# Banded attention in one program: a separate norm stage against one folded in, new engine orders, turned values

## The reference

```
x = x + attn_b(layernorm(x))           # 16 heads of 64
q = rmsnorm(x @ wq.T, q_gamma)         # over all 1024 columns of a token
k = rmsnorm(x @ wk.T, k_gamma);  v = x @ wv.T
scores = q k^T / 8 + slope_h * (j - i) # masked unless -128 <= j - i <= 0
out = softmax(scores) @ v;  attn_b = out @ wo.T
```

## Time and profile before

| what | us |
|---|---|
| median of three runs | 4155.57 |
| the three runs | 4155.28, 4165.5, 4155.57 |
| the profiled execution | 4160.83 |
| its span, first to last instruction | 4158.8 |
| TensorE busy / loads | 3639.6 / 2872.0 |
| VectorE, ScalarE, GpSimd busy | 2451.2, 1842.3, 780.7 |

### The profile page before, as it was taken

The page is one execution under the profiler, slowest core; times in us unless marked ns, Lnnn a source line. Parts: engine busy times, 40 slices in busy tenths (PEclk is TensorE's granted clock), DMA queues, the critical chain, the costliest instruction groups (busy, mean ns, idle before and its releaser), DMA issues. The chain is left out here.

```text
span 4158.8 us, 91975 instructions
## 1 busy us (share of the span) xinstructions
PE 3639.6 (88%) x33000; PEld 2872.0 (69%) x33000; DVE 2451.2 (59%) x5269; ACT 1842.3 (44%) x3752; POOL 780.7 (19%) x714
## 2 busy tenths in 40 slices
PE   4899999999966969999947899888989787899998
PEld 3566666666655858888835777777777676788887
DVE  4566666666645666666544545444545566666664
ACT  1466666666622324444413444444444232344443
POOL 0122222222210013333210000000000000233332
PEclk9999999999987979999969999999999788899999
DMA  4565556555534234333240000000000232343432
GB/s 178 145 172 170 174 172 173 168 171 174 169 123 150 86 119 122 110 108 117 75 142 33 13 13 12 13 13 13 13 13 15 87 118 93 117 122 111 115 110 44
DMA packets 383709, 424.97 MB, mean 102 GB/s; under 512 B 172864, under 2 KB 323008, under 8 KB 369728
## 3 DMA queue, kind: packets, MB, share of 16 engines
q1 hardware_dynamic: 358720, 386.04, 29.2%
q0 software_dynamic: 24576, 33.57, 4.6%
HBM read 269.24 MB, written 150.27 MB: 101 GB/s over the span
## 5 line engine op out<-in xcount | busy, mean ns | idle before, releaser
L2212 ACT ACTIVATE a_prob<-a_ps_s,a_low 128x512 f32<-128x512 f32 x512 | 318.9, 689 | 48.5 <-DVE a_low L2404 47.5
L2073 PE MATMUL a_ps_p<-a_ident,a_prob 128*128 128x128 f32 x2048 | 311.0, 285 | 14.9 <-ACT a_band L2192 9.0
L2404 DVE TENSOR_REDUCE a_low<-a_ps_s 128x2 f32<-128x1024 f32 x256 | 313.5, 1224 | 8.8
L2264 POOL TENSOR_TENSOR a_below<-a_probT,a_upper 128x512 f32<-128x512 f32 x128 | 164.3, 1284 | 726.4 <-ACT a_probT L2188 371.2
L2073 PEld LDWEIGHTS a_ps_p<-a_ident,a_prob 128*128 128x128 f32 x2048 | 217.7, 141 | 108.6 <-issue 83.3
L2188 ACT COPY a_probT<-a_ps_p 128x512 f32<-128x512 f32 x352 | 194.0, 588 | 155.6 <-PE a_ps_p L2073 155.6
L1510 ACT ACTIVATE b_prob<-b_score,b_low 128x256 f32<-128x256 f32 (+1 forms) x512 | 240.6, 473 | 23.7 <-PE b_ps_p L1452 23.7
L1462 PEld LDWEIGHTS b_ps_o<-b_v,b_probT 128*128 128x128 f32 x1792 | 227.2, 191 | 9.9 <-issue 0.9
L1583 DVE CUSTOM_DVE_ANT_0 b_score<-b_ps_s,b_bias 128x256 f32<-128x256 f32 (+1 forms) x512 | 186.0, 389 | 75.2 <-PE b_ps_s L1443 47.6
L1462 PE MATMUL b_ps_o<-b_v,b_probT 128*128 128x64 f32 x1792 | 228.2, 267 | 0.7 <-DVE b_o L1596 0.7
L2403 DVE TENSOR_TENSOR a_ps_s<-a_ps_s,a_win 128x320 f32<-128x320 f32 (+1 forms) x256 | 135.0, 527 | 140.2 <-PE a_ps_s L2106 135.7
(11 more groups left out here) (398 smaller groups left out, 10512.2 us busy)
## 6 DMA issues: line engine op xcount, KB each, us to landing
a_win<-band SPq DMA_DIRECT2D x128, 384.0 KB, 4.8
prob<-a_prob SPq DMA_DIRECT2D x128, 384.0 KB, 3.6
xnT<-n_xnT SPq DMA_DIRECT2D x32, 512.0 KB, 3.0
shift<-a_gbias SPq DMA_DIRECT2D x64, 256.0 KB, 2.4
a_shifted<-shift SPq DMA_DIRECT2D x256, 64.0 KB, 2.0
a_bins<-prob SPq DMA_DIRECT2D x128, 128.0 KB, 3.5
fe_gT<-in_WgT SPq DMA_DIRECT2D x16, 1024.0 KB
fe_uT<-in_WuT SPq DMA_DIRECT2D x16, 1024.0 KB
```

The costliest lines, as they stand in the source:

```text
L2073: last = nc.tensor.transpose(bank[:, c * P:(c + 1) * P], prob[:, t % 2, h, 32 + c * P:32 + (c + 1) * P], ident[:, :])
L2212: nc.scalar.activation(prob[:, t % 2, h, 32:32 + T], ps_s[pair][:, r, :], ACT.Exp, bias=low[:, h:h + 1]).then_inc(exped, 1)
L2264: nc.gpsimd.tensor_tensor(below[:, t % 2, :, :], probT[:, t % 2, :, t * P:(t + 1) * P], upper[:, :].unsqueeze(1).to_broadcast([P, HG, P]), ...
L2404: nc.vector.reduce_max(low[:, 2 * pair:2 * pair + 2], both[:, :, :], AX.X, negate=True).then_inc(maxed, 1)
```

## The change

- The stage n2 is no longer called. `window_stage` loads x itself, in four buffers, one a position t, and computes statistics, power, normed x, its transpose (kind `x`, through `ps_w`) and its split.
- Each of the five engines follows a list of its own, whose entries name kind, number and which tile relative to the unit's. In the place of `filled` and `emptied` there is a semaphore for each kind. The score, low and prob buffers hold eight heads instead of four.
- q and k halves: VectorE copies `ps_w` into `raw`; ScalarE squares `raw`. The two gammas are multiplied into one, `gains`, transposed at the start, and applied when VectorE empties `q_T`.
- The division by the row sum moves in front of the transposes: VectorE makes the reciprocal of two heads (`inverse`), GpSimd multiplies (`divide`), 128 x 512 at a time.
- Values: v is the weight (64 columns), the transposed probabilities stream; the output lands transposed in `ps_o`, two heads in the two halves of its partitions. `out_T` is gone. ScalarE takes the high part of the output (`high`), VectorE the rest (`rest`), and the output product is three fp32r products for each of eight chunks; wo is split for this at the start.
- Weights are split by ScalarE (high) and VectorE (rest), wo too, before the first tile's normed x. gamma is loaded as one row. The loop covers batches 2 to 6; -1 (two units), 0, 1, 7 and 8 (two units) are unrolled.

```diff
-        norm_stage(nc, "n2", ident, x2, xnT)
-        window_stage(nc, "b", ins, x2, xnT, ins["b_wqT"], ...
+        window_stage(nc, "b", ins, x2, ins["b_wqT"], ...
+WINDOW_ORDER = [
+    ("scores", 0, 0), ("x", 0, 1), ("values", 7, -1), ("scores", 1, 0), ("q", 0, 1), ("scores", 2, 0), ("out", 0, -1), ("probs_T", 0, 0),
+    ("q", 1, 1), ("probs_T", 1, 0), ("values", 0, 0), ("k", 0, 1), ("scores", 3, 0), ("k", 1, 1), ("probs_T", 2, 0), ("values", 1, 0), ("v", 0, 1),
+    ("probs_T", 3, 0), ("values", 2, 0), ("probs_T", 4, 0), ("q_T", 0, 1), ("values", 3, 0), ("probs_T", 5, 0), ("q_T", 1, 1), ("probs_T", 6, 0),
+    ("values", 4, 0), ("k_T", 0, 1), ("values", 5, 0), ("k_T", 1, 1), ("probs_T", 7, 0), ("values", 6, 0), ("v", 1, 1),
+]
+WINDOW_SCALAR_ORDER = [
+    ("x", 0, 1), ("high", 1, -1), ("exp", 0, 0), ("exp", 1, 0), ("exp", 2, 0), ("exp", 3, 0), ("q", 0, 1), ("exp", 4, 0), ("q", 1, 1), ("k", 0, 1),
+    ("exp", 5, 0), ("k", 1, 1), ("exp", 6, 0), ("v", 0, 1), ("exp", 7, 0), ("high", 0, 0), ("k_T", 0, 1), ("k_T", 1, 1), ("v", 1, 1),
+]
+WINDOW_VECTOR_ORDER = [
+    ("probs_T", 6, -1), ("x_normed", 0, 1), ("probs_T", 7, -1), ("x_stats", 0, 2), ("biased", 0, 0), ("x", 0, 1), ("biased", 1, 0),
+    ("rest", 1, -1), ("inverse", 0, 0), ("biased", 2, 0), ("q", 0, 1), ("inverse", 1, 0), ("biased", 3, 0), ("biased", 4, 0), ("out", 0, -1),
+    ("inverse", 2, 0), ("probs_T", 0, 0), ("q", 1, 1), ("inverse", 3, 0), ("x_mean", 0, 2), ("x_var", 0, 2), ("biased", 5, 0), ("k", 0, 1),
+    ("probs_T", 1, 0), ("inverse", 4, 0), ("biased", 6, 0), ("k", 1, 1), ("probs_T", 2, 0), ("inverse", 5, 0), ("mean", 0, 1), ("biased", 7, 0),
+    ("probs_T", 3, 0), ("inverse", 6, 0), ("probs_T", 4, 0), ("q_T", 0, 1), ("rest", 0, 0), ("q_T", 1, 1), ("inverse", 7, 0), ("probs_T", 5, 0),
+]
+WINDOW_POOL_ORDER = [
+    ("divide", 0, 0), ("divide", 1, 0), ("divide", 2, 0), ("x_pow", 0, 2), ("divide", 3, 0), ("divide", 4, 0), ("pow", 0, 1), ("normed", 0, 1),
+    ("divide", 5, 0), ("divide", 6, 0), ("normed", 1, 1), ("divide", 7, 0),
+]
+WINDOW_SYNC_ORDER = [("store", 0, -1), ("load", 0, 3)]
...
 # TensorE
+                elif kind == "out":
+                    pe.wait_ge(o_taken, 2 * w + 2)
+                    terms = [(c, o_part, w_part) for c in range(CH) for o_part, w_part in ((1, 0), (0, 0), (0, 1))]
+                    for c, o_part, w_part in terms:
+                        last = nc.tensor.matmul(ps_w[:, 0:C], oT[o_part][:, c, :], wo[w_part][:, c, :], ...
...
+                    elif kind == "probs_T":
+                        pe.wait_ge(divided, 8 * w + k + 1)
+                        reach(pe, copied, 8 * w + k - 1)
...
+                        for c in range(lo, 2):
+                            for r in range(2):
+                                h = 2 * k + r
+                                mm = nc.tensor.matmul(ps_o[BD * r:BD * r + BD, k % 4 * P:(k % 4 + 1) * P], v[:, at[1] - 1 + c, h * BD:(h + 1) * BD],
+                                                      probT[:, k % 2, r, c, :], start=(c == lo), stop=(c == 1), skip_group_check=True)
 # GpSimd
+                    elif kind == "normed":
+                        reach_alone(pool, pow_ready, w + 1)
+                        reach_alone(pool, raw_taken, 4 * w + 2 * k + 2)
+                        reach_alone(pool, filled["T"], 4 * w - 2 + 2 * k)
+                        nc.gpsimd.tensor_scalar(normed[:, k, :], raw[:, k, :], rrms[:, k:k + 1], 1.0, ALU.mult, ALU.mult).then_inc(normed_ready, 1)
+                    elif kind == "divide":
+                        reach_alone(pool, rinv_ready, 8 * w + k + 1)
+                        nc.gpsimd.tensor_tensor(part, part, by_row, ALU.mult).then_inc(divided, 1)
```

More of the change, by code:

```diff
@@ L1190, in _ @@
             finish(E - 1, 1, E // 2 - 1, False)
[L1193 to L1199, removed]
-WINDOW_ORDER = [
[L1206 to L1210, removed]
-]
@@ L1227, in window_stage @@
     HW = BC // HALVES
+    SECTIONS = ("x", "q", "k", "v", "q_T", "k_T", "out")
     with ExitStack() as ctx:
@@ L1287, in window_stage @@
         valued = s.sem("valued")
+        o_high = s.sem("o_high")
         o_taken = s.sem("o_taken")
         block = ctx.enter_context(s.programs())
[L1291 to L1305, removed]
@@ L1323, in section_number @@
[L1323 to L1340, removed]
@@ L1342, in uses, with tile_at, exists, steps @@
-        def uses(b, t):
-            return 2 * b + t // 2 + 1
+        def tile_at(b, t, off):
+            return b + (t + off) // NT, (t + off) % NT
+        def exists(kind, b, t):
+            return not isinstance(b, int) or 0 <= b < B
+        def steps(order, b, t):
+            for kind, k, off in order:
+                at = tile_at(b, t, off)
+                if exists(kind, *at):
+                    yield kind, k, *at
+        def rounds(engine, unit):
+            for t in range(NT - 2, NT):
+                unit(-1, t)
+            for b in range(2):
+                for t in range(NT):
+                    unit(b, t)
+            with engine.Fori(2, B - 1) as b:
+                for t in range(NT):
+                    unit(b, t)
+            for t in range(NT):
+                unit(B - 1, t)
+            for t in range(2):
+                unit(B, t)
@@ new lines, in unit @@
+            def unit(b, t):
+                for kind, _, *at in steps(WINDOW_SYNC_ORDER, b, t):
+                    if kind == "load":
+                        if not isinstance(at[0], int) or at[0] > 0 or at[1] > 1:
+                            load(*at)
+                    elif kind == "store":
+                        store(*at)
+            load(0, 0)
+            sp.dma_start(raw[0:1, :, :], gamma_d[0:1, :, :]).then_inc(gamma_in, 16)
+            for tile, dram, sem in ((ident, const["ident"], ident_in), (w_whole["q"], wqT_d, w_in["q"]),
+                                    (w_whole["k"], wkT_d, w_in["k"]), (w_whole["v"], wvT_d, w_in["v"])):
+                sp.dma_start(tile[tuple(slice(None) for _ in tile.shape)], dram).then_inc(sem, 16)
@@ new lines, in section @@
+            def section(kind, k, b, t):
+                w = number(b, t)
+                if kind == "x":
+                    pe.wait_ge(x_normed, w + 1)
+                    for c in range(KC):
+                        last = nc.tensor.transpose(ps_w[:, c * P:(c + 1) * P], xn[:, t % 2, c * P:(c + 1) * P], ident[:, :])
+                    last.then_inc(filled["x"], 1)
+                elif kind in ("q", "k", "v"):
+                    pe.wait_ge(x_split, w + 1)
+                    if isinstance(w, int) and w == 0 and k == 0:
```

498 lines of the change are left out of this document (269 added, 229 removed).

## The result

The changed kernel takes **3935.98 us** (median of 4, 3931.45 to 3943.92) beside 4155.42 for the kernel before (median of 4): a ratio of 0.9469, interval 0.9447 to 0.9492, 219 us gained where 185 were forecast. The profiled execution took 3943.92, its span is 3942.1.

What follows compares the result with a forecast made beforehand. TensorE's own program was taken to bound the kernel before, GpSimd's tail to set the pitch after. Savings of 91 (full tiles), 29 (first tiles), 7 (jumps), 55 (start) and 3 (end) sum to 185 us: median 3971, range 3920 to 4045.

Steps and rivals of the forecast that it cites:

- (a): TensorE's values product turned, two heads in two column halves: a step 0.60 us instead of 0.84, 1.9 saved a tile.
- Rival D: Column halves do not overlap: a values step stays 0.84 us, three on the path, +20, 3991 us; chance 0.09.
- rival E: Weight loads do not overlap in the turned values product: each step 1.3 us, kernel 4062; chance 0.03.
- (b), (d): TensorE, per tile: two o transposes and their ScalarE copies go (1.2 us); two x transposes are added (0.35).
- (c): Output product on TensorE as 24 fp32r products of 256 columns: about 2.85 us instead of 3.56 a tile.
- The path of a full tile: TensorE to k 1, then GpSimd's norm and divides, then TensorE: pitch 29.25 us, 3.8 saved a tile, 91 over 24.
- rival B: Divides find enough slack, only TensorE and its bank count: tiles 27.6 and 26.0 us, kernel 3922; chance 0.14.
- Rival C: GpSimd's divides are slower than their nearest row, say 2.0 us: +58, kernel 4029; chance 0.20.
- rival F: VectorE and GpSimd shut each other out of memory: divide 3.7 us, kernel about 4165, at 4 about 4190; chance 0.04.
- First tiles: First tile of each batch, with ps_w as the chain: 27.2 us against 30.78, 29 saved over eight.
- Loop jumps: Jumps of the loop over batches: 4 instead of 5, each 6.7 us in the mean, 7 saved.
- Start and end: Start: n2 goes, first scores at 42 us instead of 97.6, 55 saved; end: fewer transposes and copies, 3 saved.

Runs made afterwards that it cites:

- e3: Changed kernel with both heads of a values step writing the same half of the PSUM partitions: 4003.22 us, ratio 0.9638.
- e12: As e3, but each head's sum over its key blocks finished before the next head's began: 4006.67 us, ratio 0.9622.
- e8: Changed kernel with the output product back in f32, without the rest of o and the split of wo's rest: 3976.1 us, ratio 0.9568.
- e1: Changed kernel with each GpSimd divide treating only the first 32 columns of each head's block: 3933.76 us, ratio 0.9462.
- e2: Changed kernel with each divide done twice on GpSimd, the first into a spare buffer: 3985.61 us, ratio 0.959.
- e7: Changed kernel with the divides moved from GpSimd to VectorE, right behind each reciprocal: 3992.02 us, ratio 0.9596.
- e6: Changed kernel with its loop over batches written out: 3923.52 us, ratio 0.9432.
- e5: Kernel before the change with its loop over batches 1 to 6 written out: 4124.05 us, ratio 0.9913.
- e9: Changed kernel with the norm stage n2 put back in front of the window stage, its result unused: 3998.36 us, ratio 0.9601.
- e10: Changed kernel with 16 increments of an unused semaphore on TensorE's queue at the end of the loop body: 3938.85 us, ratio 0.947.
- e11: Changed kernel with 48 increments of an unused semaphore on TensorE's queue at the end of the loop body: 3978.62 us, ratio 0.9557.

## Why the prediction was right, and where not

**The bound.** Right: TensorE's own program sets the pace before and after, and its work per tile decides.

**(a) Values turned.** Right in mechanism and size: 0.59 for 0.60, and e3 and e12 show that the two column halves make the difference (1.02 with both heads in one). Rival D, no overlap of the halves, falls with it. So does rival E: the loads of the 64 columns last 0.136 each, eight in a step of 0.59 beside their products. The Trainium skill, page "TensorE: Matmul & The Clock Gate", section on packing small matmuls, would let them overlap only between different row groups; here the rows of the array are all in use, and the trace disagrees with it. My sum missed one thing: the four transposes ahead of a values step take 0.53, not 0.44, 0.7 us a tile.

**(b), (d).** The o transposes are gone and the x transposes cost about what was counted (the two at 2501.85 take 0.36 up to the values behind them).

**(c) Output product.** 2.92 for 2.85, in e8 0.54 less than in f32 where 0.7 were counted.

**The path of a full tile.** This step failed. "Pitch 29.25" came from GpSimd's tail; the pitch is 28.46 and comes from TensorE's work and its bank. What was mis-sized is the divide: 1.02 back to back for 1.283 + 0.27, three of them 1.6 us of the path. The waits that I named as signs did not come: 0.4 us for a divide in the whole kernel. That the number held all the same is partly luck: the two paths end within 1.1 us of each other. e1 shows that making GpSimd shorter gives nothing, e2 that it would have been the path from 1.1 us more. So rival B's mechanism is the true one. Its number, 3922, was only 14 too low because errors cancel: its batch of 3 x 27.6 + 26.0 = 108.8 measures 111.2, 19 us over the stage, and the jumps gave 17 back. Rival C, slower divides, falls with the divide's largest duration of 1.047 while VectorE is busy 62% of the stage. So does rival F, exclusion from the memory, for this kernel; but e7 shows that such a hold-up exists, 0.69 becoming 1.28 to 1.54, when VectorE multiplies two inputs in SBUF beside GpSimd. In the changed kernel VectorE's long two-input instructions in the tiles read one input from PSUM.

**First tiles.** 27.2 to 27.8 for 27.2; written out (e6) 27.2, and the tile ahead of each 27.4, since a part of the first tile's narrow work falls into it.

**Loop jumps.** This step failed too. "Each 6.7 in the mean" was read rightly for the kernel before (e5), but I took it as a property of the loop and carried it over. It is no property of the loop: unchanged, no stall, and 3.3 us over the batch; 16 increments, a stall of 1.05 that costs nothing; a stage put ahead of the loop, 2.1; the product in f32, 3.35; 48 increments, 9.5. Behind the stalls of 2 us and more the clock was low, but for one. What sets the stall is open. The changed kernel happens to be a cheap case, which is luck.

**Start and end.** 53.3 saved for 55. The weights of wo landed 12.0 after their issue and the first scores came 2.4 late; e9 puts the stage at 51.5 and the faster way to the first scores at 1 to 3.

**The 35 us.** In the spans the gain is 216.7 where the sum said 185, 32 more. From the first scores to the end of the stage it is 169.7 for 130, 40 more, and e5 and e6 take this apart. Jumps: five of 7.4 before and four of 3.3 after, 24 saved where 7 were counted, 17 more. The batches without their jumps: 129.2 to 111.2 where 130.0 (3 x 33.07 + 30.78) to 114.95 (3 x 29.25 + 27.2) was counted, 3 more in each of eight, 24. Together that is 41 of the 40. Against them stand the start with 2 less and the equal stages ahead and behind with 5.3 + 1.0 = 6 less. Against the medians it is 3 more than in the spans, because the profiled execution stood 7.9 above its median and the one before 5.3 above.

## What to carry to other kernels

An engine whose order is tight is not the path unless its slack is counted: say for each hand-over who comes first, with the producer's price at both bounds, and if half a microsecond decides, give the two cases equal chances. A cost that sits at a loop jump is no constant of the loop; read whether the engine stalls there and what clock follows, re-read it after every edit, also one of another stage, and write the loop out if the instructions fit. Before moving work to an engine, look at what runs beside it: a price read alone can double. Price a step by what stands around it: the same four transposes cost 0.44 or 0.53 by what follows, and a divide in place and back to back cost less than its nearest row.

## What was unexpected in the hardware

- A product of two inputs of 128x512 f32 on GpSimd takes 1.042 (192 of them) written in place with the short operand constant along a row, and 1.283 in the first attention; two in a row leave no gap. Which of their differences makes it faster was not tried.
- TensorE's issue stall at a loop jump was 0 in the changed kernel, 1.05 (e10), 2.0 to 2.2 (e9), 2.5 to 2.7 (before), 2.3 to 3.4 (e8) and 9.3 to 9.8 us (e11). In windows of 7 us behind the stalls of 2 us and more the granted clock was 0.50 to 0.76, and once 1.00 (behind 2.03 in e9); behind 1.03 and without a stall it was 1.00.
- A product of two SBUF inputs on VectorE takes 0.69, and 1.28 to 1.54 where it runs beside a `normed` of GpSimd (e7, 22 times); the two `normed` take 2.64 for 2.22. GpSimd's own divides never exceeded 1.047 beside VectorE in the changed kernel.
- A second head's sum begun in the same bank and on the same partitions spoiled the result while the first's was still open (e3), and not when the first was finished (e12). The two orders take the same time. The Trainium skill, page "PSUM — Partial Sum Buffer", section "The four PSUM rules", describes this: of two sums open in one bank on the same partitions, the second one's start clears the first one's marks, so that its next product overwrites instead of adding. The wrong result of e3 and the right one of e12 agree with it.
